# A new instruction order, deeper pipelining and smaller stores in a windowed-attention and router kernel

## The reference

```python
x = x + tanh(g_xattn) * xattn(layernorm(x), ctx, Wq, bq, Wk, bk, Wv, bv, Wo, bo)
x = x + tanh(g_ffn)   * ffn(layernorm(x), router_weight, router_bias, expert_bias)

def xattn(x, cond, ...):             # 8 heads of 32 channels, window of 16 positions
    q, k, v = Wq x + bq, Wk cond + bk, Wv cond + bv         # over channels
    dots[t, w] = q[t] . k[t - 8 + w] / sqrt(32)             # w = 0..15, zero padding
    out[t] = sum_w softmax_w(dots)[t, w] * v[t - 8 + w]
    return Wo out + bo

def ffn(hidden, W, b, E):            # 64 experts, one row of 2048 per channel of a sequence
    scores = softmax(hidden W^T + b)
    w = top 8 of scores, zeros elsewhere
    return hidden * sum(w) + w E
```

## Time and profile before

| what | value |
|---|---|
| median of 3 runs | 1551.26 us (1549.26 to 1552.44) |
| the profiled execution's own time | 1557.26 us |
| its span, first to last instruction | 1555.1 us |
| mean granted TensorE clock | 0.972 of full speed |
| TensorE / VectorE / ScalarE / GpSimd busy | 94% / 82% / 74% / 74% |
| read from and written to HBM | 136.88 MB, 33.55 MB |

### The profile page before, as it was taken

The page is one execution under the profiler, slowest core; times in us unless marked ns, Lnnn a source line. Parts: engine busy times, 40 slices in busy tenths (PEclk is TensorE's granted clock), DMA queues, the critical chain, the costliest instruction groups (busy, mean ns, idle before and its releaser), DMA issues.

```text
span 1555.1 us, 66658 instructions
## 1 busy us (share of the span) xinstructions
PE 1464.6 (94%) x28162; PEld 1199.9 (77%) x28162; DVE 1276.5 (82%) x2970; ACT 1144.8 (74%) x2009; POOL 1148.0 (74%) x1110
## 2 busy tenths in 40 slices
PE   4799999999999999999999999999999999999985
PEld 3687887888787888878788788878888887778764
DVE  5578987888898887988888898888889888788764
ACT  4687877777787877788787877778787787767652
POOL 4688777787777877877787887778778777677661
PEclk8899999999999999999999999999999999899896
DMA  7455455445546554454555545455554545434132
GB/s 230 125 140 126 106 173 131 123 149 143 147 121 172 141 131 146 121 157 128 149 149 141 156 119 159 128 146 147 144 159 114 159 132 142 121 98 128 44 81 85
DMA packets 365577, 210.39 MB, mean 135 GB/s; under 512 B 294497, under 2 KB 295521, under 8 KB 361057
## 3 DMA queue, kind: packets, MB, share of 16 engines
q1 hardware_dynamic: 365280, 206.14, 49.1%
HBM read 136.88 MB, written 33.55 MB: 110 GB/s over the span
## 4 chain that ended last, share of the span: by engine, by line
PE 46%; DVE 35%; issue 8%; POOL 5%; ACT 3%; DMA 2%; SPq 1%; POOLq 0%; DVEq 0%; ACTq 0%
PE ps_j L1117 18%; PE ps_s L1177 7%; PE ps_a L1142 6%; PE ps_r L1219 5%; DVE prob_t L900 5%; PE ps_s L1117 3%; DVE p_sum L890 3%; DVE st_x L907 2%; DVE wq_lo L822 2%; POOL prob L493 2%; DVE lg L1046 2%; DVE st_in L804 2%; DVE v_turn L871 2%; PE ps_s L1172 2%; PE ps_a L1196 2%
## 5 line engine op out<-in xcount | busy, mean ns | idle before, releaser
L486 POOL TENSOR_TENSOR score<-score,p_inv 128x384 f32<-128x384 f32 x256 | 221.6, 866 | 119.5 <-DVE p_inv L894 117.0
L493 POOL TENSOR_TENSOR prob<-score,prob 128x384 f16<-128x384 f32 x256 | 266.0, 1039 | 38.8 <-ACT prob L644 38.3
L1177 PEld LDWEIGHTS ps_s<-kv_win,q_col 32*32 32x32 f32 x16384 | 198.0, 107 | 57.8 <-issue 57.8
L1177 PE MATMUL ps_s<-kv_win,q_col 32*32 32x48 f32 x16384 | 234.1, 205 | 2.4 <-issue 2.2
L900 DVE STREAM_TRANSPOSE prob_t<-prob 128x512 f32<-128x512 f32 x256 | 176.7, 699 | 55.1 <-POOL prob L493 54.9
L467 POOL TENSOR_TENSOR c_lo<-c_in,c_hi 128x1024 fp32r<-128x1024 f32 x64 | 152.7, 2386 | 89.5 <-ACT c_hi L618 89.5
L1142 PEld LDWEIGHTS ps_a<-prob_t,v_diag 128*128 128x128 f16 x6528 | 175.3, 98 | 50.1 <-DVE prob_t L900 32.6
L1142 PE MATMUL ps_a<-prob_t,v_diag 128*128 128x48 f16 (+2 forms) x6528 | 187.6, 183 | 26.2 <-DVE prob_t L900 19.4
L462 POOL TENSOR_TENSOR att_lo<-att,att_hi 128x512 fp32r<-128x512 f32 x128 | 161.8, 1275 | 51.5 <-ACT att_hi L604 50.3
L1117 PE MATMUL ps_j<-c_hi,wkv_hi 128*128 128x512 f32 x512 | 171.3, 416 | 19.6 <-DVE kv_win L864 10.6
L890 DVE TENSOR_REDUCE p_sum<-score 128x8 f32<-128x384 f32 x256 | 139.2, 544 | 54.3 <-ACT score L638 53.6
(11 more groups left out here) (149 smaller groups left out, 3318.0 us busy)
## 6 DMA issues: line engine op xcount, KB each, us to landing
v_diag<-v_turn SPq DMA_DIRECT2D x512, 68.0 KB, 2.8
c_in<-ctx_dram SPq DMA_DIRECT2D x64, 512.0 KB, 4.9
x_in<-x_dram SPq DMA_DIRECT2D x64, 512.0 KB, 5.5
x_res<-x_dram SPq DMA_DIRECT2D x64, 512.0 KB, 4.3
out_dram<-x SPq DMA_DIRECT2D x32, 1024.0 KB, 7.0
c_sq<-ctx_dram SPq DMA_DIRECT2D x60, 512.0 KB, 5.5
x<-ctx_dram SPq DMA_DIRECT2D x4, 512.0 KB, 6.1
x<-experts_dram SPq DMA_DIRECT2D x2, 512.0 KB, 10.6
```

What stands on the lines that cost most here:

```text
L486: pool.tensor_tensor(score[:, u], score[:, u], p_inv[:, u, :].unsqueeze(2).to_broadcast([P, HALF, KEYS]), ALU.mult).then_inc(pm_rdy, 1)
L493: pool.tensor_tensor(part(prob[:, u % 2], 1)[:, :, 0:KEYS], score[:, u], part(prob[:, u % 2], 0)[:, :, 0:KEYS], ALU.subtract).then_inc(pl_ ...
L1177: ins = pe.matmul(s[head(h), n * KEYS:(n + 1) * KEYS], q_col[head(h), g, at:at + SUB], kv_win[c % 2][head(h), 0, g, at:at + KEYS], start=F ...
```

## The change

The arithmetic stays the same, but for how the query weight is split: the scaled weight is now written out (two ScalarE copies, into `wkv_raw[:, 0]`), rounded by a third copy over both groups, and GpSimd subtracts, where VectorE had a fused multiply and subtract per group. The rest moves work.

- **Order.** All five lists have a new order in a step. TensorE: `rows(1)` first, then `attend(0)`, `scores(0)`, `queries(1)`, `attend(1)`, `scores(1)`, the router, `scores(2)`, `output(0)`, `scores(3)`, `output(1)`, `values(0)`, `values(1)`, `rows(0)`, `queries(0)`, `keys(0)`, `keys(1)`; the mixtures stand between them, the last at the end. `normalise(3)`, `low(2)`, `low(3)`, `high(2)`, `high(3)` and the key evictions move into the next step. On VectorE `values_turn(0)` moves from the front of the step to behind `largest(3)`, and `stats_x1` ahead of `turn(1)`.
- **SP.** Loads of context first, then `v_diag` for group 0, the load of `x_in`, `v_diag` for group 1, `x_res`, and the store in four pieces of 256 KB, each as soon as its `finish(j)` is done. The square-sum load runs 6 chunks ahead, not 7. At the start the first context chunk is loaded right behind the key weight and `x_in` ahead of the query and output weights.
- **Halos.** Keys and values are copied apart, each with its own semaphores; the padding instruction `pool_pad` goes.
- **Router.** `wd` and `lg` lie in the PSUM bank `ps_r`; the sum of the router weight is one VectorE reduction and one matmul instead of 32 matmuls; the split of the experts moves from GpSimd to ScalarE and VectorE, in halves, in the first steps.
- **Semaphores.** One per unit of scores instead of one shared count.

```diff
 @@ tensor, step @@
-                if before:
-                    attend(0)
-                if now:
-                    queries(1, 0)
-                if live(b, c, -2):
-                    rows(1, -2)
-                if now:
-                    scores(0)
-                if before:
-                    attend(1)
...
-                if live(b, c, -2):
-                    router()
-                if now:
-                    scores(1)
-                    scores(2)
...
-                if before:
-                    output(0)
-                    output(1)
-                if now:
-                    scores(3)
...
+                    if live(b, c, -2):
+                        rows(1, -2)
+                    if live(b, c, -1):
+                        attend(0, -1)
+                    if live(b, c, 0):
+                        scores(0, 0)
+                        queries(1, 0)
+                    if live(b, c, -1):
+                        attend(1, -1)
+                    if live(b, c, 0):
+                        scores(1, 0)
...
+                    if live(b, c, -2):
+                        router(-2)
...
+                    if live(b, c, 0):
+                        scores(2, 0)
+                    if finishing(b, c):
+                        mixture(0)
+                    if live(b, c, -1):
+                        output(0, -1)
+                    if live(b, c, 0):
+                        scores(3, 0)
...
 @@ sync, step: the new order @@
+                if live(b, c, 0):
+                    diagonal(0)
+                if live(b, c, 5) and live(b, c, 1):
...
+                    sp.dma_start(x_in[:, :, cols(ch)], rows_in).then_inc(x_ld[ch], 16)
+                if live(b, c, 0):
+                    diagonal(1)
...
-                    rows_out = out[b - 1, g * P:(g + 1) * P, :]
-                    need(sp, fin_rdy, final(b - 1, g, NCH - 1))
-                    sp.dma_start(rows_out, x1[1 - par][:, g, :]).then_inc(out_st[g], 16)
+                    for j in range(NCH):
+                        rows_out = out[b - 1, g * P:(g + 1) * P, cols(j)]
+                        need(sp, fin_rdy, final(b - 1, g, j))
+                        sp.dma_start(rows_out, x1[1 - par][:, g, cols(j)]).then_inc(out_st[g], 16)
 @@ gpsimd @@
+                def queries_weight_low():
+
+                    need(pool, wqh_rdy, b + 2)
+                    pool.tensor_tensor(wq_lo[:], wq_ln, wq_hi[:], ALU.subtract).then_inc(wql_rdy, 1)
...
+                if live(b, c, -1):
+                    normalise(3, -1)
+                    low(2, -1)
+                if live(b, c, 0) or live(b, c, 1):
+                    halo(1, 0, vr_rdy, vleft_rdy, vl_rdy)
+                    halo(0, 0, kr_rdy, kl_rdy, kh_rdy)
+                if live(b, c, -1):
+                    low(3, -1)
 @@ router's small tiles @@
-        lg = sb("lg", [P, G, 2, E])
+        lg_rest = sb("lg_rest", [P, G, E])
-        wd = sb("wd", [P, G, E + 1])
+        wd_end = sb("wd_end", [P, G, 1])
+        wd = ps_r[:, LOGITS:LOGITS + G * E].rearrange("p (g e) -> p g e", g=G)
+        lg = ps_r[:, G * E:2 * G * E].rearrange("p (g e) -> p g e", g=G)
 @@ vector, step @@
+                if live(b, c, 0):
+                    largest(0, 0)
+                    shift(0, 0)
+                if live(b, c, 0) and live(b, c, 4):
+                    next_stats(0)
+                if live(b, c, 0) and c == 3 and seq(b + 1):
+                    ln1(b + 1)
+                if live(b, c, 0):
+                    values_turn(1, 0)
+                    total(0, 0)
+                    largest(1, 0)
+                    invert(0, 0)
+                    shift(1, 0)
...
+                    invert(1, 0)
+                    largest(3, 0)
+                    values_turn(0, 0)
+                    shift(3, 0)
+                    turn(0, 0)
+                    total(2, 0)
```

More of the change, by code:

```diff
@@ L525, in _ @@
+                if live(b, c, 0):
+                    normalise(2, 0)
+                    low(1, 0)
+                if b == -1 and c == 2:
+                    constants()
             walk(step)
@@ L856, in _ @@
-            ROUTER = 15
-            def step(b, c, par):
-                def values_low(g):
-                    rows = kv_win[c % 2][:, 1, g, OWN]
-                    need(dve, vh_rdy[g], nth(b, c, 2))
-                    dve.scalar_tensor_tensor(part(rows, 1), ps_j[g][:], v_bias[parity(c, 2, par)][:, g:g + 1],
+            values_weight_low(0, 0)
+            for ch in range(NCH):
+                dve.wait_ge(x_ld[ch], 16)
+                for g in range(G):
+                    stats_in(g, ch)
@@ new lines, in _, with values_turn, values_low @@
+            ln1(0)
+            ROUTER = 16
+            def step(b, c, par):
+                def values_turn(g, off):
+                    need(dve, vr_rdy, nth(b, c, off))
+                    need(dve, vd_ld[g], nth(b, c, off - 1) * (16 * HPG))
+                    dve.transpose(v_turn[:, g], kv_win[(c + off) % 2][:, 1, g]).then_inc(vt_rdy[g], 1)
+                def values_low(g, off):
+                    rows = kv_win[(c + off) % 2][:, 1, g, OWN]
+                    need(dve, vh_rdy[g], nth(b, c, off))
+                    dve.scalar_tensor_tensor(part(rows, 1), ps_j[g][:], v_bias[parity(c, off, par)][:, g:g + 1],
@@ L951, in step @@
                 if finishing(b, c):
                     finish(0)
-                if now:
-                    largest(2)
-                    shift(2)
+                if c == 1 and seq(b - 1):
+                    router_logits(b, 3)
+                if live(b, c, 0) and c == 1 and seq(b + 1):
+                    scales(b + 1, 1 - par, 2)
+                if live(b, c, 0):
+                    total(1, 0)
+                if live(b, c, 0) and c == 1 and seq(b + 1):
+                    scales(b + 1, 1 - par, 3)
@@ L998, in step @@
+                if live(b, c, 0):
+                    turn(1, 0)
+                if c == 1 and seq(b - 1):
                     router_weights(b, 0)
```

1114 lines of the change are left out of this document (541 added, 573 removed).

## The result

The change makes the kernel slower: 1622.04 us against 1551.85, ratio 1.0425, 95% interval 1.0395 to 1.0456. The forecast was 1527. The profiled execution of the changed kernel took 1609.19 us, the shortest of its four, so its rows show the loss at its mildest; it is 51.9 us longer than the profiled one of before (1557.26).

The account below looks back on a forecast made before the run. The prediction took TensorE, busy 94% of the span, as the bound. Its terms, -6 - 15 + 12 - 10 - 5 = -24, gave 1533 us for the profiled execution and 1527 on the median's scale, range 1500 to 1556.

Parts of the forecast that it names:

- small waits: Steady part: TensorE's waits before keys, behind the output bias and part of those before attend go, -15 us.
- The pauses called issue stay: Steady part: TensorE's pauses that nothing in the trace explains (5.3 us) stay, as the instruction count does.
- Start: Start of the kernel: most of the 6.14 us wait before the second score block and the 1.05 go, -6 us.
- late stretch: One sequence 8.4 us longer than normal, with three waits for turn there and just behind: most goes, -10 us.
- New wait in step 3: Every fourth step: scores(3), now earlier, waits for shift(1) behind ln1, 0.8 us in each of 15, +12 us.
- the 89.5 to 90 foreseen: Sign that the prediction is right: sequences in the middle take 89.5 to 90 us, none 99.
- Router tiles, halos, semaphores: Router tiles in PSUM save VectorE about 2.5 us in step 1, which it would otherwise idle: 0.
- End: Last steps and store: attend(0) waits 1.3 us instead of 3.07, twice, and the smaller last store saves 1.6: -5 us.
- That the value DMAs come late: Rival: value loads land too late for attend, some 62 steps lose 1 us each, 1589 us; chance 0.10.
- the clock below 1 in the middle: Sign that the prediction is wrong: TensorE's granted clock below 1 in the middle of the run.
- The rival of the falling clock: Rival: each new wait before scores(3) in step 3 lowers the clock and loses 3.2 us, 1575 us; chance 0.08.

Follow-up runs that it names:

- e1: The changed kernel with values_turn(0) back beside values_turn(1) and SyncE's order inside a step as in the kernel before, stores still in pieces; 1541.3 us.
- f1: The changed kernel with one instruction moved: values_turn(0) back up VectorE's order, ahead of values_turn(1), SyncE's order staying new; 1540.6 us.
- e3: The changed kernel with x_res and v_diag loaded only for the first batch item and reused for later items; 1526.1 us.
- g1: f1 with, in every fourth step alone, largest(1) and shift(1) ahead of values_turn(1), total(0) and invert(0) on VectorE; 1568.3 us.

## Why the prediction was wrong

The step that failed is one sentence under the small waits: "The pauses called issue stay, as the instruction count does." Its term was 0. It measured + 45.5 us, with + 32.4 of clock behind it. The count did stay; what moved was the traffic in which the blocks travel. The waits had 9.1 us of such pauses before (5.3 of them in the earlier trace rows), and the earlier trace rows one of 1.25 us that took the clock down, and I took them for a constant of the kernel.

**Start, -6:** right in its waits, too small in all: `attend(0)` at 62.2 in place of 70.7, - 8.5. The wait of 6.14 us became one of 0.78 (0.9 foreseen) and the 1.05 went, while a new one for a halo copy took 1.22. The sum had no term for the clock, which in the kernel before stood at 0.50 from 54.7 to 65.0 us, behind the 6.14 us wait, and in the changed one at 1.00 from 40.4.

**Small waits, -15:** right. The waits for semaphores of the earlier trace rows, 23.4 us, went down to 0.4 of `prob_t` (7.1 of them belong to the late stretch below); the list laid end to end had the order right. As these waits stood beside the pauses, part of their going may be the pauses' doing; e1 and f1, with few pauses, don't have them either.

**New wait in step 3, +12:** right in kind and near in size with the transfers gone (e3: 12.4 us in 15 waits). That it is so near is luck in part: 0.8 us was picked between 0 and 1.15. In the changed kernel it shows once, 2.0 us; I read it that the pauses ahead of it give VectorE the time. In f1 it is 22.0, as `values_turn(0)` (0.68 each) stands ahead of `shift(1)` too: 12.4 + 15 x 0.68 = 22.6.

**Late stretch, -10:** right as far as it can be seen: no wait for `prob_t` over 0.2 us in the middle. But no sequence is 90 us long. The same place in the chain of the changed kernel

```profile
428.14 4.36 PE ps_j L1119 x18
...
529.14 4.36 PE ps_j L1119 x18
```

lies 101.0 us apart, and its neighbours 98.7 and 94.9. In f1 such places are 89.9 to 94.8 apart, 91.9 in the mean from 232.06 to 1426.70. That is no less than the mean of 91.9 between the first and the last mark of the earlier trace rows, eleven sequences of the kernel before. So the 89.5 to 90 foreseen came in no kernel's mean, and what f1 gains over before lies in the start and the end.

**Router tiles, halos, semaphores, 0:** right. The operation of the earlier trace rows at a median of 1042 ns takes 288 in PSUM, and the time saved is VectorE's, which isn't the bound.

**End, -5:** half right. The last addition ends at 1604.63, 2.6 us before the span does, in place of 4.4, which is the - 1.6 of the smaller store. The waits for `prob_t` after 1450 us fell from 8.6 to 4.1 us (three waits each, of which one of 2.4 belonged to the late stretch), about as foreseen, but 4.2 us of pauses stand there that the kernel before doesn't have.

**The rivals.** That the value DMAs come late was there with 0.10, with the right place and the wrong path: `attend` waits for them 3.8 us in all (6 waits, under 1 us each), not 1 us in each step. The same lateness cost most of the 70 us through TensorE's instruction blocks, a path that I didn't have. Of what was to show the prediction wrong, the clock below 1 in the middle came true. The rival of the falling clock was right that the clock costs, but had it fall behind a new wait ahead of `scores(3)`; it fell behind the pauses. With the sum corrected by 45.5 + 32.4 the forecast would have been 1605.

## What to carry to other kernels

A kernel with many small matmuls reads its own program through the DMA engines: before moving a transfer, look at what TensorE does when it runs, and keep runs of large transfers out of the stretches with the most instructions per us. If the waits called issue cut groups of equal instructions in two, count the instructions from one to the next; if it is always the same number or a multiple of it, they are likely blocks of the program, and the transfers ahead of them are what to move. Look at the transfers of the step itself too: here a block that came late was often followed by a second, behind loads issued in between. When a wait of TensorE is taken away, check the pauses as well as the wait: in g1 the wait fell by 16 us and the pauses rose by more, for a reason that the runs show only in part.

## What the runs showed of the hardware

- TensorE's instructions arrive during the run: 223 packets of 16.4 KB for 56,264 instructions, pauses 256 instructions apart, up to 2.3 us each in the changed kernel, in the step shown with the DMA engines taken for seven tenths or more of the 2.5 us before the block's packet.
- Read from the records of the single packets in the two traces, not from a view: where 256 instructions take under 4.6 us, the next packet of q8 starts a median of about 2 us after TensorE passed the border between two blocks in the changed kernel, and about 0.9 us in the kernel before (estimates, as the borders are counted from the pauses). It takes 1.0 us in both. TensorE goes on a median of 1.4 us after the packet of the block it waits for has ended.
- A pause of 1.53 us left the clock at 1.00, one of 2.08 us that began 4 us after it had it at 0.50 for 6 us; in f1 one of 2.12 us by itself left it at 1.00. TensorE: Matmul & The Clock Gate of the Trainium skill (section HAM oscillation) tells of a clock that is lost in each round of a loop that waits for data. The trace agrees in kind, though here it is the instructions that are waited for.
